# One turn of a chunked delta-rule layer: norm and decay projection at the head, small decay operations between the masks, diagonal copies split by batch

## The chip, the cores and the metric

The kernel runs on one core of a Trainium2 chip (trn2). The metric is the device time of one execution in microseconds (us). TensorE (PE in the rows) has two levels of its clock here, 2.4 GHz, shown as a granted clock of 1.00, and 1.2 GHz, shown as 0.50. The other engines are VectorE (DVE), ScalarE (ACT), GpSimd (POOL) and SyncE (SP), which issues DMAs. Each engine runs its own instructions in order; the engines are held together only by semaphores.

## The reference

Four layers follow each other, each added to a residual. All numbers are float32. The change touches only the first, a gated delta-rule attention over 8 sequences of 256 tokens with 128 features:

```python
x = x + L0_attn(layernorm(x))      # this layer
x = x + L0_ffn(layernorm(x))       # 8 experts, 2 used, one shared
x = x + L1_attn(layernorm(x))      # softmax attention, 16 heads, and an MLP
x = x + L1_ffn(layernorm(x))       # 8 experts, 2 used, one shared
# inside L0_attn, for each token, with 16 value heads of 64:
mixed = silu(causal_conv4(h @ W_qkv.T)); q, k, v = split(mixed)
beta = sigmoid(h @ W_b.T);  g = -exp(A_log) * softplus(h @ W_a.T + dt_bias)
S = S * exp(g);  delta = (v - S k) * beta;  S = S + k delta;  o = S q
out = rms_norm(o * silu(h @ W_z.T)) @ W_out.T
```

## The kernel before, in words

The first layer is done sequence by sequence, in turns of a loop `for it in range(-2, SEQS)` (SEQS = 8) that stands once in the program of every engine. A turn works on three sequences at once: i = it in its last stage, n = it + 1 in its middle stage, f = it + 2 in its first one. `stages(it)` says which of the three exist. In it = -2 there is only f, in it = -1 n and f, in it = 6 i and n, in it = 7 only i. Nothing plans the order of the work. It is the order in which the calls are written out in the five loops, and the semaphores.

A sequence has two chunks of 128 tokens (c = 0, 1). The recurrence is turned into matrices inside a chunk. For each of eight batches k (k // 4 is the chunk, k % 4 a batch of 4 heads) the steps are:

- POOL writes a masked copy of the log decays (`masked_decays`, L502).
- TensorE sums them (`decay_sums`, L1091 and L1094, banks 0 and 1) and makes the key products (`key_products`, L1112, banks 3 to 6).
- ScalarE takes exponentials of the sums (`decay_matrix`, L615, four per batch).
- VectorE multiplies (`products`, L1866 and L1868).

Batches 0 to 2 stand at the end of the turn before. With the old order decay_sums 3 stands there too, and key products 3 open the next turn, behind decay_sums 4. decay_sums k waits for decay matrix k - 2 and key products k for products k - 2.

Then ScalarE copies the diagonal 32 x 32 blocks of the matrices to a packed tile (`diagonal_blocks`, L667, four copies per chunk, each of 32 partitions x 512). VectorE turns that tile (L1875) and inverts all blocks in 31 dependent steps (`steps_of_inverse`, L1880 and L1883), between which other VectorE work of the turn is placed. It turns the result back (L1890), and TensorE solves the larger blocks from it (L1150 and on). At the end of the turn come the convolutions of f (L1797), silus, and batches 0 to 2 of f.

The first stage of f at the head of a turn is small:

- Norm on VectorE (`prepare`), and TensorE turns it (`turn_norm`, L1029). ScalarE copies that to hT3 (`turned_norm`, L598), and TensorE projects it to beta and decay (`beta_decay`, L1038). All this is in bank 2, where `chunk_ends` (L1049 to L1051, ScalarE L624) also writes.
- VectorE makes `exponents` from it (L1809 to L1812) and ScalarE takes `exponentials` (L603).
- VectorE makes `log_decays` in three parts: 2, 9 and 8 instructions (L1820 to L1853). They form a series of small operations on 128 x 64, each of which waits for the one before.

Behind the head ScalarE applies four silus (`silu`, L645) to the value tiles of n, with a table load ahead. TensorE turns them (`v_tokens`, L1131), and before that it applies the solved matrices of i to the values (`solve`, L1224). Then come `outputs` (L1237), `end_state` (L1248, evicted by ScalarE, L741) and products from the state (`from_state`, L1259). VectorE gates the outputs (`gated`, L1911) and takes the state products (`take_state` L1940, `query_state` L1950).

The last step of a sequence is to turn its normalised heads (`turn_heads`, L1282, evicted by `turned_heads`, L758), to project them (`project_out`, L1294) and to add the input (`residual`, L1930). Chunk 1 of i has its heads turned at the end of turn i in two halves, into banks 7 and 2, and projected in the head of turn i + 1, in front of `project`, `solve` and `v_tokens`. In it = 6 and 7 the first tiles of the second layer fill gaps: `up_tile` (TensorE L1329), `gate_of_tile` (ScalarE L769), `product_of_tile` (VectorE L2010), `hidden_tiles_of` (ScalarE L775). After the loop the other three layers follow (`pair_layers`); the change leaves them as they are.

## Time and profile before

| what | us |
|---|---|
| median of three runs | 1510.51 |
| lowest of the three | 1510.26 |
| profiled execution, its time | 1512.68 |
| profiled execution, its span | 1510.9 |
| mean granted clock of TensorE over the span | 0.886 |

The span goes from the first to the last instruction in the profile, and all starts below count from its beginning. The turns with all three stages (it = 0 to 5) take 86 to 91 us each, and the last turn ends near 792 us. TensorE is busy for 1284.2 us, VectorE for 910.1 and ScalarE for 726.2. In a row of the timeline the first number is the start and the second the length of what is merged in the row; a wait in brackets is idle time of that engine just before the row, and behind the arrow stands what ended it.

### The profile page before, as it was taken

To read this page: it belongs to the slowest core of one execution; us is meant where nothing else is said; L and a number is where in the kernel's file an instruction comes from. 1 tells how busy PE (TensorE), PEld (TensorE's weight loads), DVE (VectorE), ACT (ScalarE), POOL (GpSimd) and SP (SyncE) were. 2 spreads that over 40 slices of the span, in tenths; PEclk is the share of its full clock that TensorE was granted. 3 is DMA by queue.
4 is the path that set the end of the run, shared out by engine and by line. 5 is a ranking of instruction groups with operands and counts; after the bars stand their busy time and mean duration, and the time that the engine had idled before them with its cause. 6 is when DMAs were issued, how large, how long until landed. Compare 5 with 4: busy or idle time off the path is not lost.

```text
span 1510.9 us, 26872 instructions
## 1 busy us (share of the span) xinstructions
PE 1284.2 (85%) x11048; PEld 928.8 (61%) x11048; DVE 910.1 (60%) x2365; ACT 726.2 (48%) x1353; POOL 194.1 (13%) x186
## 2 busy tenths in 40 slices
PE   2668889798898979889996959998899989989899
PEld 2355767576575756757765536665567656666566
DVE  4897888979788897969255333552445523463321
ACT  1648375665746556582541324434352354523442
POOL 5111221212112121212010010000100000000000
PEclk9768779788877978887898788998999999999999
DMA  4000000000000000010120000000000000000000
GB/s 125 4 2 5 0 2 11 2 12 1 12 1 2 11 2 8 2 32 8 54 105 8 2 1 0 1 8 1 8 0 8 1 2 8 0 1 1 1 8 7
DMA packets 15066, 17.69 MB, mean 12 GB/s; under 512 B 2567, under 2 KB 13216, under 8 KB 14560
## 3 DMA queue, kind: packets, MB, share of 16 engines
q1 hardware_dynamic: 12768, 14.09, 2.8%
q8 instruction: 87, 1.43, 0.4%
q0 software_dynamic: 576, 1.76, 0.4%
q10 hardware_dynamic: 1600, 0.12, 0.1%
q14 instruction: 35, 0.29, 0.1%
HBM read 13.87 MB, written 2.10 MB: 11 GB/s over the span
## 4 chain that ended last, share of the span: by engine, by line
PE 60%; DVE 25%; ACT 9%; issue 3%; POOL 1%; DMA 1%; SPq 0%; DVEq 0%; ACTq 0%
PE ps L1539 8%; PE ps L1529 8%; PE ps L1329 7%; PE ps L1094 4%; DVE arena L1880 4%; DVE arena L1883 3%; DVE arena L1797 3%; PE ps L1237 3%; PE ps L1112 3%; DVE arena L2154 2%; ACT arena L975 2%; PE ps L1631 2%; PE ps L1170 2%; PE ps L1595 2%; PE ps L1259 1%
## 5 line engine op out<-in xcount | busy, mean ns | idle before, releaser
L1797 DVE SCALAR_TENSOR_TENSOR arena<-ps,conv_w,arena 128x255 f32<-128x255 f32 (+2 forms) x384 | 163.8, 475 | 19.1 <-ACT arena L636 14.5
L937 ACT ACTIVATE arena<-ps 128x512 f32<-128x512 f32 x144 | 85.3, 597 | 180.7 <-PE ps L1529 180.7
L1539 PEld LDWEIGHTS ps<-arena 128*128 128x128 f32 x1152 | 132.6, 192 | 24.8 <-issue 9.9
L1539 PE MATMUL ps<-arena 128*128 128x128 f32 x1152 | 136.9, 277 | 7.1 <-ACT arena L937 4.1
L1529 PE MATMUL ps<-arena 128*128 128x512 f32 x288 | 134.3, 612 | 0.0
L2125 DVE SCALAR_TENSOR_TENSOR arena<-ps,gates,arena 128x128 f32<-128x128 f32 x128 | 36.0, 344 | 113.7 <-PE ps L1539 113.4
L523 POOL TENSOR_TENSOR rstd<-var_eps,half_power 128x2 f32<-128x2 f32 (+1 forms) x28 | 23.3, 833 | 621.1 <-DVE var_eps L1768 621.1
L2191 DVE TENSOR_REDUCE arena<-ps 128x8 f32<-128x2048 f32 (+1 forms) x24 | 54.8, 2292 | 62.8 <-PE ps L1595 62.8
L1529 PEld LDWEIGHTS ps<-arena 128*128 128x128 f32 x288 | 51.4, 194 | 61.0 <-issue 44.8
L1883 DVE TENSOR_TENSOR arena<-arena 128x30 f32<-128x30 f32 (+14 forms) x240 | 83.4, 348 | 8.2
L502 POOL TENSOR_TENSOR arena<-con,log_decay 128x512 f32<-128x512 f32 x64 | 67.0, 1059 | 162.6 <-PE ps L1094 62.1
L1880 DVE TENSOR_TENSOR arena<-arena 128x30 f32<-128x30 f32 (+14 forms) x240 | 82.6, 344 | 7.0
L2010 DVE SCALAR_TENSOR_TENSOR arena<-ps,b,arena 128x512 f32<-128x512 f32 x56 | 41.4, 749 | 70.0 <-ACT arena L769 69.8
L1079 PE MATMUL ps<-arena 128*128 128x256 f32 x256 | 75.1, 425 | 7.2 <-DVE arena L1797 6.5
L1094 PE MATMUL ps<-arena,con 128*128 128x512 f32 x128 | 79.0, 703 | 0.0
L615 ACT ACTIVATE arena<-ps,log_beta 128x128 f32<-128x128 f32 x256 | 70.6, 382 | 14.9 <-PE ps L1094 14.6
L1237 PE MATMUL ps<-arena 128*128 128x64 f32 x512 | 76.4, 319 | 0.4 <-ACT arena L727 0.4
L1237 PEld LDWEIGHTS ps<-arena 128*128 128x128 f32 x512 | 75.9, 236 | 0.9 <-ACT arena L727 0.6
L1866 DVE TENSOR_TENSOR arena<-ps,arena 128x512 f32<-128x512 f32 x64 | 44.1, 689 | 52.9 <-PE ps L1112 47.1
L517 POOL TENSOR_TENSOR o_rstd<-ssq,half_power 128x16 f32<-128x16 f32 x16 | 47.0, 2937 | 218.5 <-DVE ssq L1918 218.5
L636 ACT ACTIVATE arena<-ps,conv_w 128x256 f32<-128x256 f32 x128 | 51.7, 487 | 37.8 <-PE ps L1079 37.5
L975 ACT ACTIVATE arena<-ps 128x512 f32<-128x512 f32 x96 | 49.5, 601 | 39.4 <-PE ps L1631 39.3
(246 smaller groups left out, 2817.2 us busy)
## 6 DMA issues: line engine op xcount, KB each, us to landing
arena<-in_routed_up SPq DMA_DIRECT2D x1, 2048.0 KB, 10.5
arena<-in_routed_down SPq DMA_DIRECT2D x1, 2048.0 KB, 14.9
x_ln<-in_x SPq DMA_DIRECT2D x8, 128.0 KB, 2.3
arena<-in_w_mix SPq DMA_DIRECT2D x1, 1024.0 KB, 10.9
x_in<-in_x SPq DMA_DIRECT2D x8, 128.0 KB, 2.3
out_x<-x_res SPq DMA_DIRECT2D x8, 128.0 KB, 1.9
arena<-out_x SPq DMA_DIRECT2D x4, 256.0 KB, 2.7
out_x<-arena SPq DMA_DIRECT2D x4, 256.0 KB, 2.2
```

What stands on the lines that cost most here:

```text
L615: ins = act.activation(dm[n % 2][:, VH * c + v, :], ps[:, k % 2, h * P:(h + 1) * P], ACT.Exp, bias=log_beta[n % 2][:, c, v:v + 1])
L937: act.activation(hid1[half][:, i, :], ps[:, banks[i], :], ACT.Gelu).then_inc(s["mgelu"], 1)
L975: act.activation(probsT[u % 2][:, j, :], ps[:, 4 + j, :], ACT.Exp).then_inc(s["probs_ready"], 1)
L1079: mm = pe.matmul(ps[:, PAIR_BANK[p], j * SEQ:(j + 1) * SEQ], w_mix[:, m * P:(m + 1) * P], hT3[:, f % 3, :], start=True, stop=True)
L1094: pe.matmul(ps[:, k % 2, :], beyond, gm[k % NB], start=False, stop=True, skip_group_check=True)\
L1237: mm = pe.matmul(ps[:, (7, 5)[g], h * DH:(h + 1) * DH], dm[i % 2][:, VH * c + v, :], eps[:, v, :], start=True, stop=True)
L1329: mm = pe.matmul(ps[:, up_bank(p, k) + j, :], w[:, i * P:(i + 1) * P], hT0[:, :], start=True, stop=True)
L1529: pe.matmul(ps[:, banks[i], :], m_up[:, e, i * P:(i + 1) * P], hT_m, start=True, stop=True)\
L1539: mm = pe.matmul(ps[:, bank, c * P:(c + 1) * P], hid1[half][:, i, c * P:(c + 1) * P], m_down[:, e, i, :], start=(i == 0), stop=(i == HT1 - 1))
L1797: ins = dve.scalar_tensor_tensor(conv_tile(f, m)[:, sh:SEQ], ps[:, PAIR_BANK[p], j * SEQ:(j + 1) * SEQ - sh], conv_w[:, m, TAPS - 1 - sh:T ...
L1880: me.did(dve.tensor_tensor(tmp, inv[:, j + 1:BLOCK, j:j + 1].to_broadcast([P, rows, j]), inv[:, j:j + 1, 0:j].to_broadcast([P, rows, j]), ...
L1883: me.did(dve.tensor_tensor(inv[:, j + 1:BLOCK, 0:j], inv[:, j + 1:BLOCK, 0:j], tmp, ALU.subtract))
```

## The change

- turn_norm and beta_decay go to the head of the turn, and decay_sums 3 and decay matrix 3 of the turn before stand between and behind them. beta_decay no longer waits for chunk_ends; chunk_ends waits for exp_in_ready instead.
- exponents and the three parts of log_decays, on VectorE, go between products 2 to 6 (they stood behind products 5, behind products 7, and behind the residual). exponentials on ScalarE stands ahead of decay matrix 4.
- turn_heads and turned_heads of chunk 1 go from the end of turn i to the head of turn i + 1, between the batches, and use bank 7 for both halves; the second half waits until the first is evicted. For the last sequence they stand behind the loop.
- ScalarE's diagonal_blocks of chunk 0 stands behind decay matrix 6 instead of in front of it. That of chunk 1 is split: four copies for batches 0 to 2 (32 x 384), then four for batch 3 (32 x 128).
- Parts of the second layer's first tiles in it = 6 and 7 move with these.

```diff
--- before.py
+++ after.py
@@ -76,7 +76,7 @@
 
 
 KK_BANKS = ((3, 4), (5, 6))
-HT_BANKS = ((6, 6), (7, 2))
+HT_BANKS = (6, 7)
 V_BANKS = (2, 4)
 BA_AT = 256
 
@@ -659,12 +659,16 @@
             def diagonal_blocks(n, c):
 
                 hs = slice(VH * c, VH * (c + 1))
-                act.wait_ge(s["at_ready"], CH * NB * n + NB * (c + 1))
                 after(act, "b32_psum", 2 * n)
                 after(act, "um_blocks", QUADS * n)
-                for q in range(QUADS):
-                    r = slice(BLOCK * q, BLOCK * (q + 1))
-                    act.activation(atc[r, hs, :], at[r, hs, r], ACT.Copy).then_inc(s["atc_ready"], 1)
+
+                for lo, hi in ((0, NB),) if c == 0 else ((0, NB - 1), (NB - 1, NB)):
+                    act.wait_ge(s["at_ready"], CH * NB * n + NB * c + hi)
+                    for q in range(QUADS):
+                        r = slice(BLOCK * q, BLOCK * (q + 1))
+                        act.activation(atc[r, hs, :].rearrange("p (g y) n -> p g y n", g=2)[:, :, 2 * lo:2 * hi, :],
+                                       at[r, hs, r].rearrange("p (g y) n -> p g y n", g=2)[:, :, 2 * lo:2 * hi, :], ACT.Copy)\
+                            .then_inc(s["atc_ready"], 1)
 
             def solved32(n, c):
 
@@ -755,7 +759,7 @@
                 else:
 
                     act.wait_ge(s["y_psum"], CH * i + 1)
-                act.activation(hzT[:, 4 * j:4 * (j + 1), :], ps[:, HT_BANKS[c][j], :].rearrange("p (a b) -> p a b", b=P),
+                act.activation(hzT[:, 4 * j:4 * (j + 1), :], ps[:, HT_BANKS[c], :].rearrange("p (a b) -> p a b", b=P),
                                ACT.Copy).then_inc(s["hzT_ready"], 1)
 
             def turned_first(i):
@@ -783,18 +787,27 @@
             for it in range(-2, SEQS):
                 has_i, has_n, has_f = stages(it)
                 i, n, f = it, it + 1, it + 2
+                if has_f:
+                    turned_norm(f)
+                if has_n:
+                    decay_matrix(n, 3)
+                if has_i and i > 0:
+                    turned_heads(i - 1, 1, 0)
+                if has_f:
+                    exponentials(f)
                 if has_n:
                     decay_matrix(n, 4)
-                if has_f:
-                    turned_norm(f)
+                if has_i and i > 0:
+                    turned_heads(i - 1, 1, 1)
+                if it == SEQS - 1:
+                    hidden_tiles_of(0, 3)
+                    gate_of_tile(0, 4)
                 if has_n:
                     decay_matrix(n, 5)
                     chunk_ends(n)
+                    decay_matrix(n, 6)
                     diagonal_blocks(n, 0)
-                    decay_matrix(n, 6)
                     decay_matrix(n, 7)
-                if has_f:
-                    exponentials(f)
                 if has_n:
                     diagonal_blocks(n, 1)
                     for p in range(QK_TILES, NP):
@@ -894,21 +907,12 @@
                     decay_matrix(f, 0)
                     decay_matrix(f, 1)
                     decay_matrix(f, 2)
-                if has_i:
-                    turned_heads(i, 1, 0)
-                if it == SEQS - 1:
-                    hidden_tiles_of(0, 11)
-                if has_i:
-                    turned_heads(i, 1, 1)
-                if it == SEQS - 2:
-                    hidden_tiles_of(0, 3)
-                    gate_of_tile(0, 4)
-                if it == SEQS - 1:
-                    gate_of_tile(0, 12)
-                    gate_of_tile(0, 13)
-                    hidden_tiles_of(0, 13)
-                if has_f:
-                    decay_matrix(f, 3)
+            turned_heads(SEQS - 1, 1, 0)
+            hidden_tiles_of(0, 11)
+            gate_of_tile(0, 12)
+            turned_heads(SEQS - 1, 1, 1)
+            gate_of_tile(0, 13)
+            hidden_tiles_of(0, 13)
 
             tables = [1]
 
@@ -1024,16 +1028,13 @@
 
                 pe.wait_ge(s["d_h_ready"], f + 1)
                 after(pe, "conv_done", NP * f - 1)
-                after(pe, "hzT_ready", 4 * (f - 2))
                 for c in range(CH):
                     mm = pe.transpose(ps[:, 2, c * P:(c + 1) * P], h_tok[:, c, :], ident)
                 mm.then_inc(s["d_hT_psum"], 1)
 
-            def beta_decay(n, f, has_n):
+            def beta_decay(f):
 
                 pe.wait_ge(s["d_hT_ready"], f + 1)
-                if has_n:
-                    pe.wait_ge(s["gam_ready"], n + 1)
                 for c in range(CH):
                     mm = pe.matmul(ps[:, 2, BA_AT + 32 * c:BA_AT + 32 * (c + 1)], hT3[:, f % 3, c * P:(c + 1) * P], w_ba[:, :],
                                    start=True, stop=True)
@@ -1042,10 +1043,9 @@
             def chunk_ends(n, f, has_f):
 
                 if has_f:
-                    pe.wait_ge(s["d_hT_ready"], f + 1)
+                    pe.wait_ge(s["exp_in_ready"], f + 1)
                 pe.wait_ge(s["logdec_ready"], n + 1)
                 after(pe, "conv_done", NP * (n + 1))
-                after(pe, "hzT_ready", 4 * (n - 1))
                 pe.matmul(ps[:, 2, 0:VH], upto, log_decay[n % 2][:, 1, :], start=True, stop=True)
                 pe.matmul(ps[:, 2, VH:2 * VH], beyond, log_decay[n % 2][:, 0, :], start=True, stop=False)
                 pe.matmul(ps[:, 2, VH:2 * VH], ident, log_beta[n % 2][:, 0, :], start=False, stop=True)\
@@ -1261,7 +1261,7 @@
                         if m == QK_TILES - 1:
                             mm.then_inc(s[done], 1)
 
-            def turn_heads(i, n, c, j, has_n, has_f):
+            def turn_heads(i, c, j):
 
                 if j == 0:
                     pe.wait_ge(s["hn_ready"], CH * i + c + 1)
@@ -1271,15 +1271,13 @@
                     pe.wait_ge(s["hzT_ready"], 4 * i + 1)
                 elif j == 0:
                     pe.wait_ge(s["hz_ready"], 4 * (i + 1))
-                    if has_n:
-                        pe.wait_ge(s["u64_ready"], 4 * (n + 1))
-                elif has_f:
-                    pe.wait_ge(s["conv_done"], NP * (n + 2))
-                elif has_n:
-                    pe.wait_ge(s["vtok_ready"], 4 * (n + 1))
+                    if i + 1 < SEQS:
+                        pe.wait_ge(s["u64_ready"], 4 * (i + 2))
+                else:
+                    pe.wait_ge(s["hzT_ready"], 4 * i + 3)
                 for m in range(4):
                     at_m = 8 * j + 2 * m
-                    mm = pe.transpose(ps[:, HT_BANKS[c][j], m * P:(m + 1) * P],
+                    mm = pe.transpose(ps[:, HT_BANKS[c], m * P:(m + 1) * P],
                                       hz_slot(i, c)[:, at_m:at_m + 2, :].rearrange("p a b -> p (a b)"), ident)
                 mm.then_inc(s["hzT_psum"], 1)
 
@@ -1332,20 +1330,27 @@
             for it in range(-2, SEQS):
                 has_i, has_n, has_f = stages(it)
                 i, n, f = it, it + 1, it + 2
+                if has_f:
+                    turn_norm(f)
+                if has_n:
+                    decay_sums(n, 3)
+                if has_f:
+                    beta_decay(f)
+                if has_i and i > 0:
+                    turn_heads(i - 1, 1, 0)
                 if has_n:
                     decay_sums(n, 4)
                     key_products(n, 3)
-                if has_f:
-                    turn_norm(f)
+                if has_i and i > 0:
+                    turn_heads(i - 1, 1, 1)
+                if it == SEQS - 1:
+                    up_tile(0, 4)
                 if has_n:
                     decay_sums(n, 5)
                     key_products(n, 4)
                     chunk_ends(n, f, has_f)
                     decay_sums(n, 6)
                     key_products(n, 5)
-                if has_f:
-                    beta_decay(n, f, has_n)
-                if has_n:
                     decay_sums(n, 7)
                     key_products(n, 6)
                     key_products(n, 7)
@@ -1396,11 +1401,11 @@
                 if has_f:
                     project(f, 4, n, has_n)
                 if has_i:
-                    turn_heads(i, n, 0, 0, has_n, has_f)
+                    turn_heads(i, 0, 0)
                 if it == SEQS - 1:
                     up_tile(0, 8)
                 if has_i:
-                    turn_heads(i, n, 0, 1, has_n, has_f)
+                    turn_heads(i, 0, 1)
                 if it == SEQS - 1:
                     up_tile(0, 9)
                 if has_i:
@@ -1451,17 +1456,12 @@
                     key_products(f, 1)
                     decay_sums(f, 2)
                     key_products(f, 2)
-                    decay_sums(f, 3)
                 if it == SEQS - 1:
                     up_tile(0, 10)
                     up_tile(0, 11)
-                if has_i:
-                    turn_heads(i, n, 1, 0, has_n, has_f)
-                    turn_heads(i, n, 1, 1, has_n, has_f)
-                if it == SEQS - 2:
-                    up_tile(0, 4)
-                if it == SEQS - 1:
-                    up_tile(0, 12)
+            turn_heads(SEQS - 1, 1, 0)
+            up_tile(0, 12)
+            turn_heads(SEQS - 1, 1, 1)
             project_out(SEQS - 1, SEQS, 1, False)
             up_tile(0, 13)
 
@@ -1870,7 +1870,7 @@
             def steps_of_inverse(me, n, first, last):
 
                 if first == 0:
-                    dve.wait_ge(s["atc_ready"], 2 * QUADS * (n + 1))
+                    dve.wait_ge(s["atc_ready"], 3 * QUADS * (n + 1))
                     assert me.n == 0
                     me.did(dve.transpose(inv, atc[:, :, :].rearrange("p b i -> p i b")))
                 for j in range(max(first, 1), last):
@@ -2025,21 +2025,27 @@
                 if has_n:
                     products(me, n, 1)
                     products(me, n, 2)
+                if has_f:
+                    exponents(me, f)
+                if has_n:
                     products(me, n, 3)
+                if has_f:
+                    log_decays(me, f, 0)
+                if has_n:
                     products(me, n, 4)
+                if has_f:
+                    log_decays(me, f, 1)
+                if has_n:
                     products(me, n, 5)
                 if has_f:
-                    exponents(me, f)
+                    log_decays(me, f, 2)
                 if has_n:
                     products(me, n, 6)
                     products(me, n, 7)
-                if has_f:
-                    log_decays(me, f, 0)
+                if it == SEQS - 1:
+                    product_of_tile(0, 4)
                 if has_i and i > 0:
                     residual(i - 1, 1)
-                if has_f:
-                    log_decays(me, f, 1)
-                    log_decays(me, f, 2)
                 if has_n:
                     steps_of_inverse(lanes, n, 0, 9)
                 if has_i:
@@ -2095,7 +2101,7 @@
                     first_norm(me, 0, 0)
                     first_norm(me, 0, 1)
                     dve.wait_ge(s["w_b_in"], 16 * 10)
-                    for k in range(5):
+                    for k in range(4):
                         product_of_tile(0, k)
                 if it == SEQS - 1:
                     product_of_tile(0, 12)
```

## Rows read from the trace of the kernel before

**Rows 1.** The page: busy share of each engine, chain that ended last by engine.

```profile
PE 1284.2 (85%) x11048; PEld 928.8 (61%) x11048; DVE 910.1 (60%) x2365; ACT 726.2 (48%) x1353; POOL 194.1 (13%) x186
...
PE 60%; DVE 25%; ACT 9%; issue 3%; POOL 1%; DMA 1%; SPq 0%; DVEq 0%; ACTq 0%
```

**Rows 2.** Timeline, VectorE, head of it = 4: start, length, line, operation, [wait <- releaser].

```profile
490.99 0.69 DVE L1866 TENSOR_TENSOR arena<-ps,arena 128x512 f32<-128x512 f32 x1 [2.57 <-PE ps L1112]
...
493.00 0.69 DVE L1866 TENSOR_TENSOR arena<-ps,arena 128x512 f32<-128x512 f32 x1 [0.72 <-PE ps L1112]
...
495.48 0.69 DVE L1866 TENSOR_TENSOR arena<-ps,arena 128x512 f32<-128x512 f32 x1 [1.20 <-PE ps L1112]
...
497.75 0.69 DVE L1866 TENSOR_TENSOR arena<-ps,arena 128x512 f32<-128x512 f32 x1 [0.53 <-PE ps L1112]
...
498.96 0.68 DVE L1866 TENSOR_TENSOR arena<-ps,arena 128x512 f32<-128x512 f32 x1
...
500.15 0.18 DVE L1820 TENSOR_SCALAR sp_s<-exp_out 128x64 f32<-128x64 f32 x1
...
505.21 2.00 DVE L1875 STREAM_TRANSPOSE arena<-arena 128x1024 f32<-128x1024 f32 x1
```

**Rows 3.** Timeline, ScalarE, head of it = 4.

```profile
493.85 2.58 ACT L667 ACTIVATE arena<-arena 32x512 f32<-32x512 f32 x4
...
496.46 2.18 ACT L615 ACTIVATE arena<-ps,log_beta 128x128 f32<-128x128 f32 x8
...
502.27 1.28 ACT L645 ACT_TABLE_LOAD   x1
```

**Rows 4.** Timeline, TensorE, behind the head of it = 4.

```profile
500.82 3.68 PE L1224 MATMUL ps<-arena 128*128 128x64 f32 x32
...
505.81 1.09 PE L1131 MATMUL ps<-con,arena 128*128 128x128 f32 x8 [1.31 <-ACT arena L645]
...
514.42 2.03 PE L1259 MATMUL ps<-arena 64*128 64x128 f32 x16 [2.38 <-DVE arena L1911]
```

**Rows 5.** Stretches, L1237 alone (it = 0, 6): us, PE, PEld, PEclk, DMA share, GB/s.

```profile
151.70:158.70 7.00, 6.92 (x32) 6.82 (x32) 0.50 0.00 0
...
680.80:684.40 3.60, 3.60 (x32) 3.54 (x32) 1.00 0.02 5
```

**Rows 6.** Timeline, VectorE, it = 2 (first row) and it = 3.

```profile
334.75 0.69 DVE L1911 SCALAR_TENSOR_TENSOR arena<-ps,arena 128x512 f32<-128x512 f32 x1 [0.76 <-PE ps L1237]
...
424.75 0.69 DVE L1911 SCALAR_TENSOR_TENSOR arena<-ps,arena 128x512 f32<-128x512 f32 x1 [1.10 <-PE ps L1237]
...
429.52 0.69 DVE L1940 TENSOR_TENSOR arena<-ps,ends 128x512 f32<-128x512 f32 x1 [0.88 <-PE ps L1259]
```

**Rows 7.** Groups by line and shape, ScalarE, 481 to 517 us: count | busy, mean ns.

```profile
L615 ACT ACTIVATE arena<-ps,log_beta 128x128 f32<-128x128 f32 x32 | 8.8, 384 | 1.6 <-PE ps L1094 1.5
...
L667 ACT ACTIVATE arena<-arena 32x512 f32<-32x512 f32 x8 | 5.0, 627 | 1.0 <-DVE arena L1866 0.9
...
L598 ACT ACTIVATE arena<-ps 128x256 f32<-128x256 f32 x1 | 0.5, 454 | 0.0
...
L624 ACT ACTIVATE ends<-ps 128x32 f32<-128x32 f32 x1 | 0.2, 198 | 0.3 <-PE ps L1051 0.3
```

**Rows 8.** Timeline, TensorE, it = -1.

```profile
101.22 0.26 PE L1150 MATMUL ps<-arena 32*32 32x32 f32 x1 [11.16 <-DVE arena L1890]
```

**Rows 9.** Timeline, it = 6: TensorE's first solve, VectorE's transpose.

```profile
674.44 3.76 PE L1224 MATMUL ps<-arena 128*128 128x64 f32 x32 [0.67 <-DVE arena L1868]
...
676.34 1.96 DVE L1875 STREAM_TRANSPOSE arena<-arena 128x1024 f32<-128x1024 f32 x1 [1.85 <-ACT arena L667]
```

**Rows 10.** Timeline, TensorE and ScalarE, head and end of it = 7.

```profile
742.51 1.04 PE L1282 MATMUL ps<-con,arena 128*128 128x128 f32 x8
...
742.71 0.69 ACT L769 ACTIVATE arena<-ps,b 128x512 f32<-128x512 f32 x1 [1.32 <-PE ps L1329]
...
788.46 1.95 PE L1294 MATMUL ps<-arena 128*128 128x128 f32 x16
```

10 lines of the change are left out of this document (5 added, 5 removed).

## The prediction

> **What bounds the kernel now.** I read the page first. TensorE is busy for 85% of the span and VectorE for 60%, but the chain that ended last gives 60% to PE, 25% to DVE and 9% to ACT [rows 1]: in the first half of the run these engines wait for each other in turn. Next I read the timeline, engine by engine, at the head of one turn, it = 4 (n = 5, f = 6). On VectorE the reader is to see waits for TensorE's key products before product 3 (2.57 us), 4 (0.72 us), 5 (1.20 us) and 6 (0.53 us) [rows 2]. After product 7 come the logs of the decays, small dependent instructions from 500.15 to 505.21, and only then the transpose that opens the inverse (L1875) [rows 2]. ScalarE had its last diagonal copy done at 502.27, where its table load starts [rows 3], so that transpose waited 2.9 us longer for VectorE's own queue. The same ScalarE copy leads a second path: table load, four silus, TensorE's value transposes at 505.81 after a wait of 1.31 us, outputs, end state, and the state products (L1259) at 514.42 after a wait of 2.38 us for VectorE [rows 4]. So two paths leave the head. A is VectorE's inverse. B is diagonal copies, silu, values, outputs. The change shortens A and touches B.
>
> Which one binds differs by turn. The outputs (L1237) of seven turns ran at 1.00 of the clock in 3.6 to 3.7 us in three (it = 1, 4, 6), and at 0.50 (1.2 GHz) in 6.9 to 7.0 us in four (it = 0, 2, 3, 5); the first and the last stand in [rows 5]. In the half-clock turns path B binds: in it = 3 VectorE waits 1.10 us for the outputs and 0.88 us for the state products, in it = 2 it waits 0.76 us for the outputs [rows 6].
>
> **Path A, the logs of the decays (helps).** They move between the masks. From product 3's start (490.99) VectorE now has in its queue products 3 to 7, five times 1.2 us (498.96 to 500.15 is one of them), and all parts of the logs, 5.05 us less the 0.3 us residual that stands among them today, so 4.8 [rows 2]. With 0.2 us of gaps that is 11.0 us, so product 7 ends at about 502.0 instead of 500.15, and its first half, which the copies need, at 501.4 instead of 499.6. The waits of 0.72, 1.20 and 0.53 us cannot hide 4.8 us; only the wait of 2.57 us is large, and it takes just the exponents, since part 0 stands behind product 3. VectorE becomes full in this stretch. What goes is the serial 5.05 us behind product 7.
>
> The early norm and projection permit this. turn_norm goes ahead of decay_sums 3 and beta_decay behind it, the same TensorE work as before in a stretch where it is busy anyway, and ScalarE's exponentials end before product 3 does. I cost this at nothing; were ScalarE late, part 0 would be late by as much. turned_heads of chunk 1 goes through one bank instead of two. Its second transpose now waits for a 0.6 us eviction, which decay_sums 4 and key products 3 hide in the turns that have them (without that cover it is priced below). POOL and SP keep their order and no DMA is moved.
>
> **The diagonal copies (hurt, path B).** Chunk 0's four copies take 2.58 us from 493.85, in a hole before decay matrix 6 at 496.46 [rows 3]. Now they stand behind matrix 6. I place its sums at 494.9, its end at 496.0, the copies' end at 498.6 and matrix 7's at 499.75, where 496.46 + 2.18 was the end before [rows 3]. Chunk 1's copies are split into 384 and 128 columns, forms that the trace does not show. By the nearest rows 384 columns lie between 0.45 (256 columns) and 0.63 us (512), 128 columns between 0.20 (32 columns) and 0.38 us (128 with a bias) [rows 7]. I take 0.53 and 0.31 with their spacing, near the middle, so 2.1 and 1.25 us; the bounds for all eight are 2.6 and 4.0. The first four start behind product 6's first half (500.15) and end at 502.3, the last four at 503.55. That is 1.25 us later than 502.27 for path B, and 1.65 us earlier than 505.21 for path A. With the bounds B is 0.5 to 1.9 us later, A 1.0 to 2.4 us earlier.
>
> The Trainium skill (ScalarE: Activation LUTs, "What ACT_TABLE_LOAD costs") gives 186 ns plus 0.833 ns per element for an ACTIVATE without a pointer operand; this trace agrees, 613 ns by that against 627 ns measured for 512 columns [rows 7]. By its figures the copies would be an estimated 0.51 and 0.29 us, and a turn about 0.2 us better than I say.
>
> TensorE in addition waits about 0.8 us for product 7 before the solve (L1224), which had no wait at 500.82 [rows 4]. The values follow ScalarE anyway, so this costs nothing by itself.
>
> **What a turn gains.** In a full-clock turn the values start at 507.05, and the state products can start at about 513.4 against 514.42: 1.0 us gained. Where the inverse binds, it is 1.65. I take the middle, 1.35; VectorE is busy from there to the end of the inverse and carries it. In a half-clock turn B binds already and gets 1.25 us longer, and A's gain is worth nothing. Of the six turns with both paths and decay logs (it = 0 to 5) two ran at full clock and four at half: 2 x -1.35 + 4 x 1.25 = +2.3. Turn it = -1 has no outputs: TensorE waits 11.16 us for the inverse there [rows 8], so the whole 1.65 is gained. Turn it = 6 has no decay logs; its inverse waits 1.85 us for ScalarE [rows 9], whose last copy comes 0.5 us later by the same count (matrix 7 late, copies longer): +0.5.
>
> **The last turn and the end.** At the head of it = 7 no decay work covers the single bank. TensorE did both transposes from 742.51 without a wait; now the second waits for ScalarE, which is in a gate until 743.3 [rows 10] and evicts until 743.9: +1.05 us on a TensorE that is full there. Bounds: 0, if a later wait swallows it, and 1.6. At the very end up_tile 12 goes between the transposes, but ScalarE evicts the second only behind gate 12 (0.69 us, as its like in [rows 10]), so the projection starts at 789.2 instead of 788.46 [rows 10]: +0.75, bounds 0 and 1.5.
>
> **Sum.** +2.3 - 1.65 + 0.5 + 1.05 + 0.75 = +3.0 us (2.95). The profiled execution has a span of 1510.9 us (1512.7 timed) and the median of the runs is 1510.5; 1510.5 + 3.0 = 1513.5. About 2% of this kernel, 30 us, is what a measurement can tell from no change, and nothing here comes near it.
>
> **Rivals.**
> *Full clock everywhere.* If outputs run at 1.00 in all six turns, A binds. Each gains about 1.5, and the four half-clock ones lose the waits they have now, 0.8 us in the two like it = 2 and 2.1 in the two like it = 3: 6 x 1.5 + 2 x 0.8 + 2 x 2.1 = 14.8. With -1.65 + 0.5 + 1.8 = +0.65 that is -14, 1496.5. For it: the wait of 2.38 us before the state products nearly goes. Against it: nothing shortens the wait before the values, behind which the clock fell in four turns. The Trainium skill (TensorE: Matmul & The Clock Gate, "Why this matters for your kernels") warns only of idle gaps longer than these; by that rule no outputs should be at 0.50, and this rival would be the forecast. The outputs at 0.50 [rows 5] disagree with it.
>
> *Half clock everywhere, the side above.* VectorE's late product 7 puts a new idle gap of 0.8 us before the 64-column solve, beside the old one behind it, and the clock falls ahead of the outputs in all six turns. The two full-clock turns then get 1.25 us plus 0.8 to 2.1 us of such waits, +2.7 each: 4 x 1.25 + 2 x 2.7 + 0.65 = +11, 1521.5. With four half-clock turns of six the sum is above zero, with three it is about zero; that is the point from which it decides. For it: four of seven are at 0.50 now. Against it: it = 6 has a gap of 0.67 us before the solve already [rows 9] and kept full clock [rows 5].
>
> *The moved logs free nothing*, because ScalarE is later than I think and the inverse starts when it did: the gains of 1.35 and 1.65 fall away: 4 x 1.25 + 0.5 + 1.8 = +7, 1518.
>
> **How the numbers follow.** The forecast (a mix as now, two to three full turns) 0.5, with 1506 to 1519 as its own range; full clock in most turns 0.22; half clock in all 0.2; logs free nothing 0.05; the rest 0.03. Turns change their place against the clock's changes, and each that flips moves the time by 3 to 4 us. Range 1499 to 1524. Faster by over 2% would need 4 us in every turn: 0.03; slower by as much 0.03; within 2% 0.94.
>
> **What would show it.** Right, in turns it = 0 to 5: L1875 about 12.6 us behind the start of product 3 (14.2 now), with ScalarE's copies ending its wait; product 7 1.8 us later; values 1.25 us later behind the silus; a new wait before L1224; outputs at 0.50 in about four turns; in it = 7 a wait of about 1 us between the two halves of L1282. Wrong: product 7 on time, values not late, or outputs at 1.00 in five or more turns, and then the time is below 1506; or an inverse that starts less than 1 us earlier, and then it is above 1516.

## The result, and the profile after

| what | before | changed |
|---|---|---|
| median of five runs, us | 1510.26 | 1520.94 |
| lowest of five, us | 1502.88 | 1515.67 |
| profiled execution, its time, us | 1512.68 | 1515.67 |
| profiled execution, its span, us | 1510.9 | 1513.9 |
| mean granted clock | 0.886 | 0.891 |

One of the five runs of the kernel before took 2404.46 us, a slow one that the ratio leaves out. The ratio is 1.008, with an interval of 1.0052 to 1.0108, so the change costs 8 to 16 us, clear of no change though far under 2%. The forecast was 1513.5 in a range of 1499 to 1524. The two profiled spans differ by 3.0 us only, and neither stands in the middle of its runs: the changed kernel's profile is the lowest of its five, and that of the kernel before is above all of its runs but the slow one. A profile is one draw here, and I took a second one of each kernel below.

The page of the changed kernel, the same lines as in [rows 1]:

```profile
PE 1281.5 (85%) x11040; PEld 925.2 (61%) x11048; DVE 912.7 (60%) x2365; ACT 734.0 (48%) x1385; POOL 197.2 (13%) x186
...
PE 54%; DVE 29%; ACT 11%; issue 4%; POOL 1%; DMA 1%; SPq 0%; DVEq 0%; ACTq 0%
```

The busy times of TensorE and VectorE are the same within 0.3%, and ScalarE's is 8 us longer, with 32 more instructions. In the chain PE has lost 6 points, and DVE, ACT and issue have gained them: more of the time that ended last runs through VectorE and ScalarE.

VectorE at the head of it = 4 in the changed kernel, which answers to [rows 2] (start, length, line, operation, [wait <- releaser]):

```profile
485.92 0.69 DVE L1866 TENSOR_TENSOR arena<-ps,arena 128x512 f32<-128x512 f32 x1 [1.38 <-PE ps L1112]
...
488.27 0.69 DVE L1866 TENSOR_TENSOR arena<-ps,arena 128x512 f32<-128x512 f32 x1 [0.37 <-PE ps L1112]
...
491.65 0.68 DVE L1866 TENSOR_TENSOR arena<-ps,arena 128x512 f32<-128x512 f32 x1
...
494.31 0.69 DVE L1866 TENSOR_TENSOR arena<-ps,arena 128x512 f32<-128x512 f32 x1
...
495.51 0.68 DVE L1866 TENSOR_TENSOR arena<-ps,arena 128x512 f32<-128x512 f32 x1
...
496.10 0.68 DVE L1868 TENSOR_TENSOR arena<-ps,arena 128x512 f32<-128x512 f32 x1
...
498.62 1.98 DVE L1875 STREAM_TRANSPOSE arena<-arena 128x1024 f32<-128x1024 f32 x1 [1.64 <-ACT arena L669]
```

The rows are products 3, 4, 5, 6 and 7 (its two halves) and the transpose. Between 488.27 and 496.78 there is no wait: VectorE is full, as the prediction said. Product 3 starts at 485.92 and product 7 ends at 496.10 + 0.68 = 496.78, 10.9 us later. Before it was 9.2 us. The transpose comes 12.7 us behind product 3's start (14.2 before) and now waits 1.64 us for ScalarE's copies (L669, L667 before).

ScalarE in the same stretch, against [rows 3]:

```profile
490.06 1.14 ACT L615 ACTIVATE arena<-ps,log_beta 128x128 f32<-128x128 f32 x4 [0.89 <-PE ps L1094]
...
491.07 2.56 ACT L669 ACTIVATE arena<-arena 32x512 f32<-32x512 f32 x4
...
493.66 1.14 ACT L615 ACTIVATE arena<-ps,log_beta 128x128 f32<-128x128 f32 x4
...
495.11 3.48 ACT L669 ACTIVATE arena<-arena 32x384 f32<-32x384 f32 x8 [0.31 <-DVE arena L1866]
...
498.61 1.28 ACT L645 ACT_TABLE_LOAD   x1
```

Matrix 6 now comes before chunk 0's four copies (491.07) and matrix 7 behind them. Chunk 1's eight copies take 3.48 us, chunk 0's four whole ones 2.56. By shape, over the whole run, the columns are count | busy, mean ns, as in [rows 7]:

```profile
L669 ACT ACTIVATE arena<-arena 32x384 f32<-32x384 f32 x32 | 16.6, 520 | 2.9 <-DVE arena L1866 2.4
...
L669 ACT ACTIVATE arena<-arena 32x128 f32<-32x128 f32 x32 | 9.8, 307 | 0.8
```

TensorE behind it, against [rows 4]:

```profile
492.99 0.70 PE L1112 MATMUL ps<-arena 64*128 64x256 f32 x4 [0.52 <-DVE arena L1868]
...
496.93 3.76 PE L1224 MATMUL ps<-arena 128*128 128x64 f32 x32 [0.40 <-DVE arena L1868]
...
502.14 1.09 PE L1131 MATMUL ps<-con,arena 128*128 128x128 f32 x8 [1.46 <-ACT arena L645]
...
503.07 3.68 PE L1237 MATMUL ps<-arena 128*128 128x64 f32 x32
...
508.48 1.16 PE L1259 MATMUL ps<-arena 64*128 64x128 f32 x16
```

There are new waits for VectorE: 0.52 us before the last key products and 0.40 us before the solve (L1224). The values (L1131) start 16.2 us behind product 3's start (502.14 less 485.92) against 14.8 before (505.81 less 490.99). The state products (L1259) have no wait any more, where they had 2.38 us: path A no longer binds there, path B does. The first 32 outputs (L1237) of this turn ran at full clock. In it = 3 the same stretch looks like this:

```profile
411.93 1.39 PE L1131 MATMUL ps<-con,arena 128*128 128x128 f32 x8 [1.45 <-ACT arena L645]
...
413.12 6.93 PE L1237 MATMUL ps<-arena 128*128 128x64 f32 x32
...
422.90 1.16 PE L1259 MATMUL ps<-arena 64*128 64x128 f32 x16
```

The 32 products of the outputs take 6.93 us here, at a granted clock of 0.50. In it = 4 they took 3.68 us at 1.00.

A full-clock turn is below one whose first 32 outputs ran at 1.00, a half-clock turn one where they ran at 0.50. From product 3's start to VectorE's query products (L1950) a full-clock turn of the changed kernel takes 28.0 us (513.93 less 485.92) and a half-clock one 31.4. Before it was 29.0 to 29.2, and 30.0 to 31.3. **Up to that point a half-clock turn of the changed kernel costs 3.4 us more than a full one, before it cost 0.8 to 2.1.**

Whole turns, from product 3's start to the next turn's, say less. Over both profiles of each kernel (the second ones come below) and without it = 0, full-clock turns took 86.5 to 86.8 us before, 86.7 in the mean of five, and 85.3 to 86.9 changed, 86.2 in the mean of four; it = 4 of the first profile is left out, where the second chunk's outputs lost the clock. Half-clock turns took 87.5 to 89.8 before and 88.4 to 91.3 changed, 88.4 and 89.9 in the means of five. So a whole full-clock turn gained 0.5 us and not 1.2, and a half-clock one lost 1.5. Part of what a full-clock turn gained is lost at the head of the next. Key products 2 behind a full-clock turn, before (it = 3, second profile) and changed (it = 4, second profile):

```profile
482.32 0.70 PE L1112 MATMUL ps<-arena 64*128 64x256 f32 x4
...
572.57 1.23 PE L1112 MATMUL ps<-arena 64*128 64x256 f32 x4
```

From product 2's end to product 3's start it was 1.9 us behind every full-clock turn before (it = 1 to 5), at a granted clock of 0.90 to 0.92 from product 0 on. Changed it was 2.1 us behind one of the four full-clock turns and 2.8 to 3.1 behind three, whose clock there was 0.73 to 0.75.

The two places at the end of the attention, where one bank had to do, against [rows 10]:

```profile
745.57 0.66 PE L1280 MATMUL ps<-con,arena 128*128 128x128 f32 x4 [0.83 <-ACT arena L762]
...
791.77 1.49 PE L1292 MATMUL ps<-arena 128*128 128x128 f32 x11 [0.69 <-ACT arena L762]
```

### The profile page after: what moved, and what is told of

It reads as the page before. It is cut to its first block, busy times and chain, and to the rows that moved or that the text cites. A ratio compares the mean times of both kernels' runs of the same rounds, so it can differ in the third digit from the quotient of the medians.

```text
span 1513.9 us, 26879 instructions
## 1 busy us (share of the span) xinstructions
PE 1281.5 (85%) x11040; PEld 925.2 (61%) x11048; DVE 912.7 (60%) x2365; ACT 734.0 (48%) x1385; POOL 197.2 (13%) x186
## 4 chain that ended last, share of the span: by engine, by line
PE 54%; DVE 29%; ACT 11%; issue 4%; POOL 1%; DMA 1%; SPq 0%; DVEq 0%; ACTq 0%
PE ps L1539 8%; PE ps L1529 8%; PE ps L1327 7%; DVE arena L1797 5%; DVE arena L1880 4%; DVE arena L1883 4%; PE ps L1237 3%; PE ps L1094 3%; ACT arena L979 3%; DVE arena L2160 2%; PE ps L1112 2%; PE ps L1595 2%; ACT arena L669 2%; PE ps L1631 2%; PE ps L1079 1%
## 5 line engine op out<-in xcount | busy, mean ns | idle before, releaser
L1797 DVE SCALAR_TENSOR_TENSOR arena<-ps,conv_w,arena 128x255 f32<-128x255 f32 (+2 forms) x384 | 163.9, 476 | 20.9 <-ACT arena L636 16.4
L941 ACT ACTIVATE arena<-ps 128x512 f32<-128x512 f32 x144 | 85.2, 597 | 179.1 <-PE ps L1529 179.0
L1539 PEld LDWEIGHTS ps<-arena 128*128 128x128 f32 x1152 | 132.6, 192 | 24.8 <-issue 9.9
L1529 PEld LDWEIGHTS ps<-arena 128*128 128x128 f32 x288 | 50.8, 192 | 59.9 <-issue 44.2
L615 ACT ACTIVATE arena<-ps,log_beta 128x128 f32<-128x128 f32 x256 | 72.1, 371 | 29.1 <-PE ps L1094 28.8
L1079 PE MATMUL ps<-arena 128*128 128x256 f32 x256 | 79.0, 444 | 8.1 <-DVE arena L1797 7.2
L1237 PE MATMUL ps<-arena 128*128 128x64 f32 x512 | 72.7, 309 | 0.4 <-ACT arena L731 0.4
L1237 PEld LDWEIGHTS ps<-arena 128*128 128x128 f32 x512 | 72.3, 226 | 1.0 <-ACT arena L731 0.6
L1112 PE MATMUL ps<-arena 64*128 64x256 f32 x256 | 52.0, 503 | 24.6 <-DVE arena L1797 20.7
L1224 PE MATMUL ps<-arena 128*128 128x64 f32 x512 | 66.5, 291 | 6.0 <-DVE arena L1868 5.6
## 6 DMA issues: line engine op xcount, KB each, us to landing
arena<-in_routed_up SPq DMA_DIRECT2D x1, 2048.0 KB, 11.1
arena<-in_routed_down SPq DMA_DIRECT2D x1, 2048.0 KB, 15.6
arena<-in_w_mix SPq DMA_DIRECT2D x1, 1024.0 KB, 11.1
```

What stands on the lines that cost most here:

```text
L615: ins = act.activation(dm[n % 2][:, VH * c + v, :], ps[:, k % 2, h * P:(h + 1) * P], ACT.Exp, bias=log_beta[n % 2][:, c, v:v + 1])
L941: act.activation(hid1[half][:, i, :], ps[:, banks[i], :], ACT.Gelu).then_inc(s["mgelu"], 1)
L1079: mm = pe.matmul(ps[:, PAIR_BANK[p], j * SEQ:(j + 1) * SEQ], w_mix[:, m * P:(m + 1) * P], hT3[:, f % 3, :], start=True, stop=True)
L1112: mm = pe.matmul(ps[:, KK_BANKS[k % 2][g], 0:2 * P].rearrange("p (q n) -> p q n", q=2), mix_qk[n % 2][r:r + DH, QK_TILES + b, cs], mix_qk[ ...
L1237: mm = pe.matmul(ps[:, (7, 5)[g], h * DH:(h + 1) * DH], dm[i % 2][:, VH * c + v, :], eps[:, v, :], start=True, stop=True)
L1529: pe.matmul(ps[:, banks[i], :], m_up[:, e, i * P:(i + 1) * P], hT_m, start=True, stop=True)\
```

## Experiments

Each kernel and the kernel before ran side by side on one chip, in three groups on three chips. The columns behind the ratio come from its profile; the three positions count from product 3's start, in a turn with all three stages (it = 1 to 5). "Half clock" is the number of the seven turns it = 0 to 6 in which the 32 first outputs (L1237 or its line there) took over 6.4 us.

| kernel | median us | ratio, interval | product 7 ends | values start | inverse starts | half clock |
|---|---|---|---|---|---|---|
| before, first profile | 1510.26 | 1 | 9.2 | 14.8 | 14.0 to 14.2 | 4 |
| before_again | 1509.62 | 0.9992 [0.9972, 1.0012] | 9.2 | 14.8 | 13.9 | 4 |
| changed, first profile | 1520.94 | 1.0080 [1.0052, 1.0108] | 10.9 | 16.2 | 12.7 | 3 |
| after_again | 1521.99 | 1.0078 [1.0054, 1.0102] | 10.9 | 16.2 | 12.7 | 4 |
| undo_diag | 1528.00 | 1.0105 [1.0068, 1.0142] | 10.9 | 16.4 | 12.9 | 5 |
| logs_behind | 1525.57 | 1.0098 [1.0077, 1.0120] | 10.3 | 15.8 | 15.0 | 7 |
| before_diag | 1517.81 | 1.0054 [1.0035, 1.0074] | 10.0 | 15.6 | 14.7 | 6 |
| after_oldpos | 1519.80 | 1.0080 [1.0055, 1.0104] | 10.9 | 16.2 | 12.7 | 5 |
| spread_newpos | 1522.34 | 1.0093 [1.0067, 1.0120] | 10.2 | 15.7 | 12.2 | 7 |
| logs_spread | 1493.42 | 0.9886 [0.9854, 0.9919] | 9.4 | 14.8 | 11.3 | 0 |
| before_fill | 1508.57 | 0.9996 [0.9975, 1.0017] | 9.2 | 16.0 | 13.9 | 0 |
| before_fill1 | 1510.97 | 1.0015 [0.9998, 1.0032] | 9.2 | 14.8 | 13.9 | 0 |
| spread_fill | 1494.79 | 0.9893 [0.9862, 0.9925] | 9.4 | 15.8 | 11.2 | 0 |
| spread_fill1 | 1496.97 | 0.9929 [0.9909, 0.9949] | 9.4 | 14.8 | 11.2 | 0 |

The theory was the prediction's own: both moved pieces stand ahead of product 7, and what hangs on product 7 (copies, silu, values, outputs) is later in every turn. The rivals were that only one of the pieces costs anything, and that the cost is the clock's draw alone.

### The two kernels again

> The kernel before, unchanged, for a second profile of it. Theory (which clock a turn's outputs get is drawn anew in each execution, the work is the same): the ratio is 1.00 within 0.004; product 7 ends 9.2 us behind the start of product 3 and the values start 14.8 us behind it in every turn as in the first profile, but the half-clock outputs stand in other turns or in another number of them than four of seven. Rival (the clock's pattern belongs to the program): half clock again in it = 0, 2, 3 and 5.

> The changed kernel, unchanged, for a second profile of it. Theory (path B, from the copies to the values, is later in every turn, and the profiled execution was the luckiest of five): ratio 1.008, values 16.2 us behind product 3's start against 14.8, and more of the seven outputs at half clock than the three or four of the first profile. Rival (the change costs the 3 us that the two profiles differ by and the rest is scatter): ratio 1.002 to 1.004.

The positions inside a turn came back to 0.1 us, and the ratio came back. The half-clock turns of the kernel before were now it = 0, 2, 4 and 6 instead of 0, 2, 3 and 5, so their place is drawn anew; the rival that it belongs to the program falls. In it = 6 the same gap of 0.67 us before the solve stood ahead of full-clock outputs in the first profile and of half-clock ones in the second. The changed kernel had four half-clock turns instead of three, where more than four were expected, and this profile too was the lowest of its runs. Its span was 1516.2 against 1508.7 us, 7.5 apart where the first pair was 3.0 apart. By the ratios, 1.0080 and 1.0078, the kernels are 12 us apart both times.

Every run's mean granted clock was taken beside its span, not only the profiled ones', and that settles what part a worse draw of the clock had. At 0.885 eight runs of the kernel before have spans of 1510.4 to 1515.8 us, and three of the changed one 1522.6 to 1523.3. From 0.888 to 0.891 the changed kernel's four spans fall from 1519.1 to 1513.9, and the medians of the kernel before from 1509.4 to 1505.1. At an equal mean clock the two are thus some 9 to 11 us apart. The rival that the cost is the clock's draw alone falls; the lower mean clock of the changed kernel, 0.887 against 0.890, goes with the remaining few us.

### One piece undone at a time

undo_diag, on the changed kernel:

```diff
                     chunk_ends(n)
+                    diagonal_blocks(n, 0)
                     decay_matrix(n, 6)
-                    diagonal_blocks(n, 0)
                     decay_matrix(n, 7)
...
-                for lo, hi in ((0, NB),) if c == 0 else ((0, NB - 1), (NB - 1, NB)):
-                    act.wait_ge(s["at_ready"], CH * NB * n + NB * c + hi)
+                act.wait_ge(s["at_ready"], CH * NB * n + NB * (c + 1))
```

> The changed kernel with the diagonal copies as before: chunk 0's ahead of decay matrix 6, chunk 1's in four whole ones. The logs stay between the products. If the late values come from VectorE's full queue (product 7 about 1.7 us late), four whole copies behind it make the values later still: 16.6 to 16.8 us behind product 3's start, against 16.2 with the change, and the ratio to the kernel before is 1.009 to 1.013. If the late values come from the copies' new place and split, they come back to 15.0 us and the ratio falls to 1.000 to 1.003.

logs_behind, on the changed kernel:

```diff
                 if has_n:
                     products(me, n, 3)
-                if has_f:
-                    log_decays(me, f, 0)
...
+                if has_f:
+                    log_decays(me, f, 0)
                 if has_i and i > 0:
                     residual(i - 1, 1)
+                if has_f:
+                    log_decays(me, f, 1)
+                    log_decays(me, f, 2)
```

> The changed kernel with the three parts of the decay logs behind product 7 again (the exponents stay early). If VectorE's full queue delays the values, product 7 comes back to 9.2 us behind product 3's start, the values to 15.6 (the copies' place and split still cost 0.8), and the inverse starts 14.2 behind it as before: ratio 1.002 to 1.005. If the earlier inverse is worth more than the earlier values, this kernel is above the changed one, 1.010 or more.

Neither helped. With the copies as they were, product 7 stays at 10.9 us: VectorE's queue alone holds it there. The values came at 16.4 us, later than with the change as expected, but by 0.2 and not 0.4 to 0.6; the ratio is in the expected range. With the logs out of the way it comes back only to 10.3, not to the 9.2 I expected, because ScalarE makes matrix 7 late. I had worked out that delay of 1.1 us in the prediction and then left it out of this expectation. The values at 15.8 are close to the 15.6 expected, and the ratio missed: 1.0098 instead of 1.002 to 1.005. The reason stands in TensorE's rows of it = 1 in this kernel:

```profile
239.99 3.76 PE L1224 MATMUL ps<-arena 128*128 128x64 f32 x32 [0.60 <-DVE arena L1868]
...
245.34 1.19 PE L1131 MATMUL ps<-con,arena 128*128 128x128 f32 x8 [1.60 <-ACT arena L645]
...
246.33 6.93 PE L1237 MATMUL ps<-arena 128*128 128x64 f32 x32
```

There is a gap of 0.60 us before the solve, one of 1.60 us before the values, and then the outputs at half clock. The gap before the solve was 0.60 us in all of it = 1 to 5, and the outputs were at half clock in all seven turns.

before_diag has the change to the copies alone, place and split, on the kernel before (as in the change's own diff, at both places):

> The kernel before with the change to the diagonal copies alone: chunk 0's behind decay matrix 6, chunk 1's split 3 + 1. If the copies' place alone delays the values, product 7 ends 10.3 us behind product 3's start (9.2 before) and the values start 15.6 to 15.8 us behind it (14.8), with no gain in return since the logs still end last on path A: ratio 1.004 to 1.010. If the change's cost comes from VectorE's queue, product 7 stays at 9.2 and the ratio is 0.998 to 1.002.

VectorE in it = 4 (n = 5) of that kernel, products 3 and 7 and the transpose:

```profile
493.21 0.69 DVE L1870 TENSOR_TENSOR arena<-ps,arena 128x512 f32<-128x512 f32 x1 [2.67 <-PE ps L1116]
...
501.91 0.69 DVE L1870 TENSOR_TENSOR arena<-ps,arena 128x512 f32<-128x512 f32 x1 [0.65 <-ACT arena L615]
...
502.52 0.68 DVE L1872 TENSOR_TENSOR arena<-ps,arena 128x512 f32<-128x512 f32 x1
...
508.17 1.99 DVE L1879 STREAM_TRANSPOSE arena<-arena 128x1024 f32<-128x1024 f32 x1
```

Product 7 waits 0.65 us for decay matrix 7, where it had no wait before, and ends 10.0 us behind product 3's start. The transpose still stands behind the logs, and they behind product 7: a loss on both paths, 1.0054. So the copies' change costs by itself. Its place holds back product 7, and the split was not tried alone.

### Both pieces off product 7's way

logs_spread cuts the logs into six and puts only as much ahead of product 7 as VectorE's waits hold; the last two pieces, nine small instructions, stand beside ScalarE's copies. It also puts chunk 0's copies ahead of matrix 6:

```diff
                 if has_f:
                     exponents(me, f)
+                    log_decays(me, f, 0)
                 if has_n:
                     products(me, n, 3)
                 if has_f:
-                    log_decays(me, f, 0)
+                    log_decays(me, f, 1)
                 if has_n:
                     products(me, n, 4)
                 if has_f:
-                    log_decays(me, f, 1)
+                    log_decays(me, f, 2)
                 if has_n:
                     products(me, n, 5)
                 if has_f:
-                    log_decays(me, f, 2)
+                    log_decays(me, f, 3)
...
                     residual(i - 1, 1)
+                if has_f:
+                    log_decays(me, f, 4)
+                    log_decays(me, f, 5)
```

> The changed kernel with chunk 0's diagonal copies ahead of decay matrix 6 again (the split stays), and with the logs cut into six parts that fit VectorE's waits: the first ahead of product 3, 0.2 to 1.0 us each behind products 3, 4 and 5, the last two behind product 7, beside ScalarE's copies. If the cost of the change is only that both pieces lie ahead of product 7, product 7 ends 9.3 to 9.8 us behind product 3's start, the values start 14.6 to 15.2 behind it, the inverse 11.7 to 12.5: ratio 0.992 to 0.998. If early norm, early exponents and the single bank cost something of their own, values stay above 15.6 and the ratio is above 1.002.

VectorE in it = 3 of this kernel, product 3, product 6, product 7's second half, the transpose:

```profile
388.22 0.69 DVE L1868 TENSOR_TENSOR arena<-ps,arena 128x512 f32<-128x512 f32 x1
...
395.15 0.69 DVE L1868 TENSOR_TENSOR arena<-ps,arena 128x512 f32<-128x512 f32 x1 [0.80 <-PE ps L1112]
...
396.95 0.68 DVE L1870 TENSOR_TENSOR arena<-ps,arena 128x512 f32<-128x512 f32 x1
...
399.47 1.96 DVE L1877 STREAM_TRANSPOSE arena<-arena 128x1024 f32<-128x1024 f32 x1
```

And TensorE behind it:

```profile
397.81 3.73 PE L1224 MATMUL ps<-arena 128*128 128x64 f32 x32
...
402.99 1.09 PE L1131 MATMUL ps<-con,arena 128*128 128x128 f32 x8 [1.46 <-ACT arena L645]
...
403.92 3.68 PE L1237 MATMUL ps<-arena 128*128 128x64 f32 x32
...
409.33 1.16 PE L1259 MATMUL ps<-arena 64*128 64x128 f32 x16
```

Product 7 ends 9.4 us behind product 3's start, the transpose starts at 11.3 (earlier than the 11.7 to 12.5 expected), the solve has no wait, the values start at 14.8 as before the change. That is A shortened by 2.7 to 2.9 us and B untouched. The ratio of 0.9886 is below the expected 0.992 to 0.998. Whole turns say where the gain lies: 85.3 to 85.5 us in it = 1 to 4, which is 1.3 us under a full-clock turn of the kernel before and 2 to 4.5 under its half-clock ones. No turn's outputs were at half clock, and I take that for the part that the expectation lacked; it is not separated from the rest.

spread_newpos is the same with chunk 0's copies behind matrix 6, four instructions later in ScalarE's queue:

> logs_spread with chunk 0's diagonal copies behind decay matrix 6, as in the change. logs_spread had the inverse 11.2 us and the values 14.8 us behind product 3's start. If the copies' place is a cost of its own, product 7 is 0.7 to 1.0 us later, and so are inverse and values (15.6): the ratio goes from 0.989 to 0.993 to 1.000. If the place only hurts together with late logs, the ratio stays at 0.987 to 0.991.

```profile
404.28 0.69 DVE L1868 TENSOR_TENSOR arena<-ps,arena 128x512 f32<-128x512 f32 x1
...
413.20 0.69 DVE L1868 TENSOR_TENSOR arena<-ps,arena 128x512 f32<-128x512 f32 x1 [1.11 <-ACT arena L615]
```

```profile
414.64 3.75 PE L1224 MATMUL ps<-arena 128*128 128x64 f32 x32 [0.60 <-DVE arena L1870]
...
419.99 1.69 PE L1131 MATMUL ps<-con,arena 128*128 128x128 f32 x8 [1.60 <-ACT arena L645]
```

The first fence is VectorE in it = 3, products 3 and 7, the second TensorE's solve and values. Product 7 waits 1.11 us for ScalarE, and the gaps of 0.60 and 1.60 us are back. The ratio of 1.0093 misses both expectations (0.993 to 1.000, 0.987 to 0.991), and the median is 29 us above that of logs_spread. The later product 7 explains 0.8 us a turn, some 6 us. Most of the rest is seen in the outputs: half clock in seven turns against none, and 30.8 to 32.4 us from product 3's start to the query products in it = 1 to 5 against 26.6 in logs_spread.

after_oldpos is the changed kernel with chunk 0's copies ahead of matrix 6, logs and split as changed:

> The changed kernel with chunk 0's copies ahead of decay matrix 6; logs in three coarse parts ahead of product 7, split kept. If VectorE's full queue alone keeps product 7 at 10.9 us behind product 3's start, moving the copies gives back only what ScalarE saves behind it: values 15.7 to 16.0 (16.2 with the change), ratio 1.004 to 1.008. If the copies' place was the main cost, values at 15.0 and ratio below 1.002.

Product 7, values and ratio are those of the changed kernel. While VectorE's queue holds product 7 at 10.9 us, it doesn't matter when ScalarE has matrix 7. Product 7 is the later of two arrivals, and each piece of the change delays one of them. Only it = 6, which has no logs, got its product 7 and values back (9.5 and 14.8 us against 10.3 and 15.8).

### The clock, filled by hand

before_fill puts three extra products in the idle gap ahead of the values, on the kernel before. Their results are overwritten by the transposes that follow:

```diff
                 if c == 0 and j == 0:
-                    pe.wait_ge(s["v_silu"], (NP - QK_TILES) * (n + 1))
                     pe.wait_ge(s["gam_ready"], n + 1)
                     if has_f:
                         pe.wait_ge(s["exp_in_ready"], f + 1)
+                    for _ in range(3):
+                        pe.matmul(ps[:, 2, :], ident, con[:, 0:512], start=True, stop=True)
+                    pe.wait_ge(s["v_silu"], (NP - QK_TILES) * (n + 1))
```

> The kernel before, with three extra fp32 products of 512 columns on TensorE (their result is overwritten) in the idle gap of 1.3 us ahead of the value transposes. If that gap makes the clock fall ahead of the outputs, the outputs run at full clock (3.7 us) in all or nearly all of seven turns against three or four of seven; each turn that is turned is 2 to 3 us shorter, and the ratio is 0.993 to 0.997. If the clock falls for another reason (the 64-column products themselves), the outputs stay at 6.9 us in three or more turns, the extra products cost up to 1.3 us at half clock, and the ratio is 1.000 to 1.004.

> The kernel before with one extra product instead of three. Three of them took 2.6 us at full clock instead of the 1.3 that they were meant to, and made the values 1.15 us late. One takes 0.86 us and fits into the gap. If what the three gained by the full clock was eaten by the late values, the values now stay at 14.8 us, most outputs are at full clock and the ratio is 0.994 to 0.998. If 0.45 us of gap is still enough to let the clock fall, three or more turns are at half clock and the ratio is 0.998 to 1.002.

TensorE in it = 3 with three, and then with one of them; L1124 is the extra product, each recorded as two:

```profile
407.92 3.68 PE L1226 MATMUL ps<-arena 128*128 128x64 f32 x32
...
411.44 2.79 PE L1124 MATMUL ps<-con 128*128 128x512 f32 x6
...
414.07 1.04 PE L1133 MATMUL ps<-con,arena 128*128 128x128 f32 x8
...
414.94 1.23 PE L1239 MATMUL ps<-arena 128*128 128x64 f32 x10
```

```profile
410.70 1.08 PE L1124 MATMUL ps<-con 128*128 128x512 f32 x2
...
412.17 1.09 PE L1133 MATMUL ps<-con,arena 128*128 128x128 f32 x8 [0.39 <-ACT arena L645]
...
413.10 3.12 PE L1239 MATMUL ps<-arena 128*128 128x64 f32 x27
```

I had sized the filler wrongly: three took 2.79 us instead of 1.3 and made the values 1.15 us late. In it = 0 they made them 4.1 us late (19.0 against 14.9). One takes 1.08 us, and the values are on time. In both kernels the outputs of all seven turns were at full clock, against four of seven at half clock in both profiles of the kernel before. The other runs agree: their mean granted clock was 0.897 to 0.905 with three extra products and 0.894 to 0.904 with one, against 0.883 to 0.895 in the kernel before beside them. So in this kernel work in the gap before the values keeps the clock up for the outputs. But the time did not follow: 0.9996 and 1.0015, where 0.993 to 0.997 and 0.994 to 0.998 were expected. In the kernel before, path A binds right behind the outputs, and VectorE's query products came 29.1 to 29.2 us behind product 3 in it = 1 to 5 of before_fill1, where full-clock turns had 29.0 to 29.2 and half-clock ones 30.0 to 31.3; so 0.8 to 2.1 us were to be had in each half-clock turn. Whole turns of before_fill1 took 86.6 to 87.7 us in it = 1 to 4 and 89.5 in it = 5, none clearly below the 86.7 of full-clock turns without the filler. Where that time went is open.

> The kernel logs_spread with the same three extra products ahead of the values. If gap and clock hang together: outputs at full clock in all turns, path A binds in all of them, ratio 0.985 to 0.992. If not: equal to logs_spread or up to 0.004 above it.

> logs_spread with one extra product ahead of the values. The outputs of logs_spread were at full clock in seven of seven turns in its profile already, so filling the gap should give little: ratio 0.986 to 0.990 against 0.989. If logs_spread's profile was a lucky one and half-clock turns are usual in it, the gain is larger: 0.982 to 0.986.

On logs_spread there is nothing to fill, since its outputs were at full clock already. The filler gained nothing: 0.9893 with three products, the same as logs_spread within the intervals, and 0.9929 with one, above both expectations. The 0.9893 fits both of its expectations and decides nothing. In it = 0 of spread_fill1 the outputs took 4.53 us, at 0.80.

## Why the prediction was right or wrong

The number was inside the range and the direction right, but the sum said +3 us and the measured cost is 12: most of it was missed. The positions inside the head were right, what they do to a whole turn was not.

**Path A (right).** Product 7 was predicted to end 11.0 us behind product 3's start and ended at 10.9. The new copies were taken as 0.53 and 0.31 us and took 0.520 and 0.307. The transpose was predicted at 12.6 and came at 12.7, with ScalarE ending its wait.

**Path B (right, a little small).** Values 1.25 us later predicted, 1.4 measured. The idle time before the solve was predicted as 0.8 us; 0.52 us of it fell before the last key products and 0.40 before the solve.

**A full-clock turn (right to the query products, too large for the turn).** -1.35 us predicted; 28.0 against 29.2 to the query products is -1.2. The prediction let VectorE carry that through the turn. Whole turns show -0.5 in the mean: in three of four the clock was lower at the next head, which the sum did not have.

**A half-clock turn (direction right, a little small).** +1.25 us predicted. To the query products 31.4 against 30.0 is +1.4 in turns like it = 2 before, and against 31.3 it is +0.1 in turns like it = 3. Whole turns show +1.5 in the mean. By these two means a mix of two full-clock and four half-clock turns makes +5 us, an estimate, where the sum had +2.3.

**"A mix as now" (not contradicted by the profiles).** Three and four of seven against four: the change did not bring more half-clock turns in its two profiles. Both were the lowest of their runs, though. after_oldpos has the same positions in it = 1 to 5 and the same ratio as the changed kernel, and its profile shows five half-clock turns and a span of 1523.5; those with three and four have 1513.9 and 1516.2. The rival "half clock everywhere", at 1521.5, is nearest to the median of 1521, and that is luck as far as the profiles show. Its new gap before the solve came, but half clock in all six turns came with it only in logs_behind and spread_newpos. The argument held against it, that it = 6 has such a gap and kept full clock, rested on one draw: in before_again it = 6 was at half clock.

**Turn it = -1 (mis-sized).** -1.65 us predicted. From its key products 0 to the next turn's it was 72.7 against 73.0 us, and 73.9 against 74.8 in the second pair: -0.4 and -0.9. The inverse did gain 1.5 us against product 3's start. But the early norm, costed at nothing, did cost here: turn_norm and beta_decay now stand ahead of key products 3, and these came 7.62 us behind key products 0 instead of 6.80. In the other turns chunk 1's turned heads stood there before as well, and key products 3 lost little.

**The last two turns (sum right, one term small).** +0.5 + 1.05 + 0.75 = +2.3 predicted. From the key products 0 of it = 6 to the last residual of the attention (L1930) it was 137.9 against 134.9 us, and 138.4 against 136.2: +3.0 and +2.2. The waits for ScalarE are there, 0.83 and 0.69 us. The +0.5 was too small: without any logs, product 7 ended 10.3 us behind product 3's start in it = 6 instead of 9.1, and the inverse started at 12.3 instead of 11.1, +1.1. Matrix 7 behind the copies holds back product 7 there too: with the copies ahead of it, in after_oldpos, product 7 of it = 6 ended at 9.5.

**The sum.** +3.0 us predicted. The pairs of profiles say +3.0 and +7.5, the runs +12 us (8 to 16). The direction held. The first pair's +3.0 meets the sum by luck, since the changed kernel's profile was its lowest run. What failed is the size of the terms for whole turns: with -0.5 and +1.5 in place of -1.35 and +1.25, and the measured ends, an estimate comes to +7. The other 5 us stay open. A lower clock can't be all of it, since 9 to 11 us remain between runs of equal mean clock, and only profiled executions show their turns.

**"Full clock everywhere"** fell: three and four half-clock turns of seven. The Trainium skill (TensorE: Matmul & The Clock Gate, "Why this matters for your kernels") warns only of longer idle gaps than those of 1.3 to 1.6 us here. It doesn't say that shorter ones are harmless, and the filled kernels show that they are not: with the 1.31 us gap the kernel before had the outputs of it = 1 to 5 at half clock in three and in two of five turns, and with 0.39 us of the gap left in none.

**"The moved logs free nothing"** fell: the inverse starts 1.5 us earlier.

## What to carry to other kernels

A small chain of dependent operations hides only in waits at least as long as itself. Measure each wait, cut the chain to their lengths, and put the rest beside another engine's work behind the last operation that others wait for; the 19 small instructions had a part in a loss of 0.8% when cut into three lumps, and in a gain of 1.1% when cut into six. Work moved ahead of an operation that two queues feed must be checked in both queues: taking away one of the two delays gained nothing here, taking away both made the fastest kernel of the study, 1.1% (some 17 us) below the one before. And where TensorE idles for a microsecond around small products, price the clock into the step and take several profiles.
